# Second products of a routed-expert loop: high and low weights side by side in one 512-column product

## The chip, the cores and the metric

The kernel runs on one core of a Trainium2 chip. The metric is the device time of one execution in microseconds (us); the kernel before has a median of 1322.04 us over 3 runs.

## What is computed

The input x is (2, 2048, 256) in float32: 4096 rows of 256 features. The reference runs four residual layers one after the other: a linear attention, a mixture of experts, a causal attention, and the same mixture again with the same weights. Each mixture is

```python
xn = layernorm(layernorm(x)) * ln_gamma + ln_beta
abel_out = gelu(xn @ abel_w + abel_b)                 # dense branch, 256 -> 256
topw, topi = top_k(xn @ moe_gate_w + moe_gate_b, 2)   # 8 experts, 2 per row
h  = gelu(xn @ ew1[e] + eb1[e])                       # 256 -> 512
eo = h @ ew2[e] + eb2[e]                              # 512 -> 256
moe_out = (sum of the 2 weighted eo) @ expm(gens[0]) @ expm(gens[1]) @ expm(gens[2])
gate = sigmoid([abel_out, moe_out] @ gc_w + gc_b)
x = x + norm(x) + abel_out * (1 - gate) + moe_out * gate
```

## The kernel before, in words

**Stages.** `weights()` prepares the weights, `context()` does the linear attention, then come `mixture(0)`, `attention`, and `mixture(1)`. The three rotations are folded into the experts' second weights `ew2`. Products that must be exact use a pair of reduced-precision operands: a float32 value is kept as a high part that the engine's fast float32 format (`f32r`) holds exactly and a low part, the rest. A product is then high rows by high weights, high rows by low weights, and low rows by high weights.

**The expert loop.** Each mixture sorts its 8192 (row, expert) pairs by expert into `SLOTS` = 71 tiles of 128 rows, so there are 142 tiles in two loops (in the profile 312 to 570 us and 1005 to 1268 us). `over_tiles` runs a loop's first 7 tiles as straight code, then 7 turns of a hardware loop with 8 tiles each, then the last 8 as straight code. Engines are programmed by hand and run each its own order; semaphores bind them. For tile j:

- GpSimd (`gpsimd`, L1482 to L1496) fetches tile j+4 of x from the DRAM tensor `slots_in` once `back_ok` says that tile j is done with its ring slot, and then scatters the results of tile j (L1495) once `zy_ok` of tile j is there. It takes them in this order, so the fetch of tile j+5 stands behind the scatter of tile j.
- TensorE (`run_tiles`, L1887) does `up(j)` (6 products of 512 columns, `split` L1838, with first weights), `turn_x(j+1)` (2 transposes, L1851), `down_first(j-1)` (6 products of 256 columns), `turn_h(j)` (4 transposes, L1868) and `down_second(j-1)` (6 products of 256 columns). `split` issues L1842 (high by high), L1843 (high by low) and L1844 (low by high), for the first and for the second weights alike, each with a weight load of its own (the rows are the stationary operand, the expert's weights the moving one).
- ScalarE: Gelu of `up(j)` into `hid` (L1673), then the high part of x for tile j+1 (`high_x`, recorded as L207), then, after `turn_h`, the high part of the turned Gelu rows (recorded as L202).
- VectorE (`step`, L1388): the low part of x for tile j+1 (`copy_x`, L1357), the low part of the turned Gelu rows of tile j (L1394), and then for tile j-1: a register read of the expert number, the sum of PSUM and the expert's bias into `yr` (`results_part`, L1378), a product with the gate vector that is summed up (`gate_part`, L1385); at last two small ones for the scatter addresses of tile j+1 (`route_back`, L1366 and L1369). In the second mixture `aside` puts two products of the dense branch (L1255) behind them in tiles 1 to 6.

So the order that VectorE keeps is: L1394 of tile j, the results of tile j-1, the addresses, L1357 for tile j+2. `up(j+2)` waits for that L1357, `turn_h` waits for Gelu, and `down_first(j)` waits for L1394 of tile j.

**Banks.** The second product of tile j has the first 256 columns of PSUM bank 6 or 7 (by parity of j); the other 256 are unused.

**Memory.** `ew1` and `ew2` hold the high parts of all 8 experts. The low parts lie in DRAM and are fetched per expert by SyncE (`fetch_weights`, L1511) into one of four places, `low1_in` and `low2_in`; that of expert e+4 goes where e's was, once the tiles of e are through. `low2_in` lies under the first half of `ab`, the dense branch's result. In the second mixture `ew2` is fetched too (`high2`), since the attention used its place. `ew2` is laid out by chunk first, `[P, HC, E, C]`, so an expert's share is 4 pieces of 1 KB per partition.

Of the kernel before, what the change touches and what calls it, by code (L numbers as in the profile page):

```python
# [20 lines left out]
P = 128  # L21
# [8 lines left out]
def build(nc, d, out):  # L30
# [7 lines left out]
    NT = T // P  # L38
# [16 lines left out]
    with ctx:  # L55
# [28 lines left out]
        xh = sb("xh", [P, NT, CW])  # L84
        keys = under("keys", [P, BT // GT, 2, KC, BANK], F32)
# [3 lines left out]
        values = under("values", [P, BT // GT, 2, GT, C], F32)  # L89
        ew2 = sb("ew2", [P, HC, E, C])  # L90
# [73 lines left out]
        wqkv = flat(ab)[:, NT * C - KC * 3 * HD:].rearrange("p (c n) -> p c n", c=KC)  # L164
# [14 lines left out]
        def turn_half(pe, n, b):  # L179
            e, hs = half(n)  # L180
            for c in range(KC):
                for h in range(HH):
                    last = pe.transpose(bank[:, b, (c * HH + h) * P:(c * HH + h + 1) * P],
                                        ew2[:, hs.start + h, e, c * P:(c + 1) * P], ident[:])
            return last
# [27 lines left out]
        def weights():  # L213
# [9 lines left out]
            a3 = Arena(flat(ab)[:, GT * C:])  # L223
# [51 lines left out]
            with nc.Block() as block:  # L275
                @block.sync
                def _(sp):
# [28 lines left out]
                    for c in range(HC):  # L306
                        sp.dma_start(ew2[:, c, :, :], d["L0_ffn_ew2"][:, c * P:(c + 1) * P, :].rearrange("e p h -> p e h")
# [471 lines left out]
        ctx_arena = Arena(flat(ab))  # L779
# [21 lines left out]
        def context():  # L801
# [28 lines left out]
            with nc.Block() as block:  # L830
                @block.sync
                def _(sp):

                    sp.dma_start(turning, R.rearrange("p c j -> p (c j)")).then_inc(st_high, 16)
                    for e in range(E):
# [5 lines left out]
                        if e % 2:  # L841
                            sp.dma_start(high2[e // 2].rearrange("p (h c) -> p h c", h=HC), ew2[:, :, e // 2, :]).then_inc(st_high, 16)
# [17 lines left out]
                def _(v):  # L860
# [11 lines left out]
                    def rest_second(n):  # L872
# [4 lines left out]
                        v.tensor_tensor(rest2[n % 4], bank[:, FY[n % 2], :].rearrange("p (h c) -> p h c", h=HH), ew2[:, hs, e, :],  # L877
# [42 lines left out]
                def _(act):  # L920
# [10 lines left out]
                    def folded(n):  # L931
                        e, hs = half(n)
                        act.wait_ge(fold_Y, n + 1)
                        copy(act, f32r(ew2[:, hs, e, :]), bank[:, FY[n % 2], :].rearrange("p (h c) -> p h c", h=HH)).then_inc(fold_ok, 1)
# [101 lines left out]
        def mixture(r):  # L1036
# [86 lines left out]
            RETURNED = ((xs, xs_out), (ab, ab_out)) if r == 1 else ((xs, xs_out),)  # L1123
# [125 lines left out]
            def vector(v):  # L1249
                def dense_gate(g, some=range(GT)):  # L1250

                    v.wait_ge(gelu_ok, step_of[g] + 1)
                    for t in some:
                        after(v, zab_ok, gated(g) - GT + t)
                        v.scalar_tensor_tensor(prod, ab[:, g * GT + t, :], 1.0, gcw[:, 1, :], ALU.mult, ALU.mult,  # L1255
# [3 lines left out]
                def rest_late(n):  # L1259
# [4 lines left out]
                    v.tensor_tensor(late_rest[n % 2], bank[:, fold_bank(n), :].rearrange("p (h c) -> p h c", h=HH), ew2[:, hs, e, :],  # L1264
# [114 lines left out]

                def gate_part(j, k):  # L1380

                    v.wait_ge(y_ok, past + j + 1)
# [5 lines left out]
                def step(j, k, turn):  # L1388
# [18 lines left out]
                results_part(SLOTS - 1, (SLOTS - 1) % RING, (SLOTS - 1) // RING)  # L1407
                gate_part(SLOTS - 1, SLOTS - 1)
# [15 lines left out]
                def last_tile(g, k):  # L1424

                    if 0 <= g < NG:
# [5 lines left out]
                        src = (ab[:, g * GT + t, :], q[:, t, 0, 0:C], q[:, t, 1, 0:C])[k]  # L1432
# [65 lines left out]
            def sync(sp):  # L1498
# [7 lines left out]
                def spill_dense(p):  # L1506
                    g = ORDER[p]
                    sp.wait_ge(gelu_ok, p + 1)
                    sp.dma_start(ab_out[g], ab[:, tiles(g), :].rearrange("p t c -> p (t c)")).then_inc(spilled[g % 4], 16)

                def fetch_weights(e):  # L1511
# [58 lines left out]
                for e in range(LOWS, E):  # L1570
                    fetch_weights(e)
                    if r == 0:
# [4 lines left out]
                        sp.dma_start(high2[e].rearrange("p (h c) -> p h c", h=HC), ew2[:, :, e, :]).then_inc(late_high, 16)  # L1577
                if r == 0:
                    prepared.sync(sp)
                for g in range(LOWS):  # L1580
# [4 lines left out]
                    for o, i in RETURNED:  # L1585
                        sp.dma_start(o[:, tiles(g), :].rearrange("p t c -> p (t c)"), i[g]).then_inc(spilled[g], 16)
# [916 lines left out]
```

## Time and profile before

| | us |
|---|---|
| median of 3 runs | 1322.04 |
| lowest and highest | 1310.57, 1322.39 |
| the profiled execution's own time | 1321.78 |
| its span, first to last instruction | 1320.0 |
| first expert loop, from its first product to its last results | 312 to 570 |
| second expert loop | 1005 to 1268 |

The profile is of one execution. PE is TensorE's products, PEld its weight loads (which run beside products), DVE VectorE, ACT ScalarE, POOL GpSimd, SP SyncE. A row of the timeline has start, duration, engine, line, operation and operands, and in brackets the idle time before it with what ended it. Ends of products are modelled, so the spacing of starts is what counts. "issue" is a wait that no semaphore in the profile explains. Tensor names in rows leave out digits, so `ew` is `ew1` or `ew2`, and `low_in` is `low1_in` or `low2_in`.

### The profile page before, as it was taken

The page shows a single profiled execution, that of the slowest core. Times are in us where ns is not written, and L with a number is a line of the kernel's source. Part 1 is how long each engine was busy: PE and PEld are TensorE (multiplying, and loading weights), DVE is VectorE, ACT ScalarE, POOL GpSimd, SP SyncE. Part 2 cuts the span into 40 slices and gives each one's busy share as a digit, 9 for nine tenths or more (in the row PEclk, how much of TensorE's full clock was granted, in tenths as well). Part 3 has the DMA queues.
Part 4 walks back from the last instruction along what each step waited for, and adds up shares of the span by engine and source line. Part 5 has one row for each costly group of instructions (what it writes and reads, how often), then busy time and mean ns, then how long its engine had stood idle before and what let it go on. Part 6 is the DMA issues. An engine that isn't in the chain of part 4 may idle for free.

```text
span 1320.0 us, 25866 instructions
## 1 busy us (share of the span) xinstructions
PE 1166.6 (88%) x7208; PEld 1012.9 (77%) x7209; DVE 861.9 (65%) x2758; ACT 494.8 (37%) x961; POOL 415.0 (31%) x494
## 2 busy tenths in 40 slices
PE   7988968888999999945999989999994999999958
PEld 6746657776888899934789878888873889899947
DVE  6668767756666666655876667766672766666646
ACT  1104624244444444422333333343542444444435
POOL 3003116872444444410000000105573444444410
PEclk8998968779999999976999999998896999999979
DMA  9401314445444533360011100001247534433357
GB/s 295 140 8 65 128 64 156 160 161 181 133 140 138 162 96 88 93 224 0 1 49 49 49 20 30 1 1 65 97 165 240 188 120 124 120 105 111 105 189 256
DMA packets 72271, 149.15 MB, mean 113 GB/s; under 512 B 10918, under 2 KB 36210, under 8 KB 72186
## 3 DMA queue, kind: packets, MB, share of 16 engines
q1 hardware_dynamic: 51626, 92.87, 20.3%
q0 software_dynamic: 19776, 54.45, 13.7%
q8 instruction: 42, 0.69, 0.2%
q10 hardware_dynamic: 784, 0.79, 0.2%
q14 instruction: 43, 0.35, 0.1%
HBM read 82.63 MB, written 65.44 MB: 112 GB/s over the span
## 4 chain that ended last, share of the span: by engine, by line
PE 52%; issue 11%; DVE 7%; POOL 7%; DMA 5%; ACT 2%; POOLq 1%; SPq 1%; DVEq 0%; ACTq 0%
PE bank L2301 18%; PE bank L1842 6%; PE bank L1843 6%; PE bank L1844 6%; POOL slots_in L1474 4%; PE bank L1868 3%; PE bank L1706 3%; PE bank L1921 3%; DMA xh<-slots_in 2%; PE bank L2359 2%; POOL xh L1484 2%; PE bank L1851 2%; POOLq L1483 1%; POOL results L1495 1%; PE bank L2312 1%
## 5 line engine op out<-in xcount | busy, mean ns | idle before, releaser
L1842 PE MATMUL bank<-ew,rows 128*128 x852 | 298.2, 350 | 5.8 <-DVE rows L1357 3.8
L1843 PE MATMUL bank<-low_in,rows 128*128 x852 | 273.6, 321 | 0.0
L1844 PE MATMUL bank<-ew,rows 128*128 x852 | 272.2, 319 | 0.0
L1495 POOL DMA_INDIRECT results<-xh x142 | 143.2, 1009 | 293.7 <-DVE xh L1385 275.5
L1842 PEld LDWEIGHTS bank<-ew,rows 128*128 128x128 f32 x852 | 161.4, 189 | 17.0 <-issue 9.7
L1844 PEld LDWEIGHTS bank<-ew,rows 128*128 128x128 f32 x852 | 161.0, 189 | 11.4
L1673 ACT ACTIVATE xh<-bank 128x512 f32<-128x512 f32 x142 | 85.1, 599 | 219.3 <-PE bank L1844 219.3
L1843 PEld LDWEIGHTS bank<-low_in,rows 128*128 128x128 f32 x852 | 162.0, 190 | 6.2
L1394 DVE TENSOR_TENSOR rows<-bank,rows 128x512 fp32r<-128x512 f32 x142 | 98.2, 692 | 93.2 <-ACT rows L202 93.2
L1474 POOL DMA_INDIRECT slots_in<-xh,work x120 | 118.1, 984 | 78.3 <-DVE work L1236 44.7
L723 POOL TENSOR_TENSOR work<-work,mhalf 128x8 f32<-128x8 f32 x24 | 39.6, 1649 | 323.7 <-DVE work L716 311.0
L202 ACT ACTIVATE rows<-bank 128x512 fp32r<-128x512 f32 x142 | 85.1, 599 | 77.2 <-PE bank L1868 77.2
L2301 PE MATMUL bank<-values,shares 128*128 128x256 f32 x816 | 111.5, 288 | 1.9 <-DVE shares L2106 1.9
L2301 PE MATMUL bank<-keys,queries 128*128 128x512 f32 (+2 forms) x480 | 107.7, 377 | 0.0
L1706 PE MATMUL bank<-abw,work 128*128 128x8 f32 (+1 forms) x512 | 102.5, 348 | 3.9 <-ACT work L207 2.1
L2301 PEld LDWEIGHTS bank<-values,shares 128*128 128x128 f32 x816 | 101.7, 190 | 4.4 <-DVE shares L2106 3.6
L1706 PEld LDWEIGHTS bank<-abw,work 128*128 128x128 f32 x512 | 88.2, 216 | 13.8 <-ACT work L207 2.8
L2301 PEld LDWEIGHTS bank<-keys,queries 128*128 128x128 f32 x480 | 85.9, 195 | 13.6
L1378 DVE TENSOR_TENSOR xh<-bank,work 128x256 f32<-128x256 f32 x142 | 60.3, 425 | 49.8 <-issue 46.7
L1357 DVE SCALAR_TENSOR_TENSOR rows<-bank,rows 128x256 fp32r<-128x256 f32 x142 | 60.3, 424 | 41.4 <-ACT rows L207 38.0
L1484 POOL DMA_DIRECT2D xh<-slots_in x142 | 78.5, 553 | 27.8 <-issue 26.8
L1868 PE MATMUL bank<-ident,xh 128*128 128x128 f32 x568 | 85.6, 273 | 0.7 <-ACT xh L1673 0.7
(347 smaller groups left out, 2016.2 us busy)
## 6 DMA issues: line engine op xcount, KB each, us to landing
xh<-slots_in POOLq DMA_DIRECT2D x142, 129.0 KB, 2.6
low_in<-low SPq DMA_DIRECT2D x32, 512.0 KB, 5.0
xh<-results SPq DMA_DIRECT2D x14, 1032.0 KB, 5.4
dense<-ab SPq DMA_DIRECT2D x12, 512.0 KB, 7.2
xs<-in_L_attn_a_x_dram SPq DMA_DIRECT2D x4, 1024.0 KB, 8.4
ew<-in_L_ffn_ew_dram SPq DMA_DIRECT2D x2, 2048.0 KB, 13.3
ew<-in_L_ffn_ew_dram SPq DMA_DIRECT2D x4, 1024.0 KB, 14.4
low<-xh SPq DMA_DIRECT2D x8, 512.0 KB, 2.7
```

The costliest lines, as they stand in the source:

```text
L202: return eng.activation(o, i, ACT.Copy, scale=scale)
L1394: v.tensor_tensor(f32r(q[:, 1]), bank[:, 4 + k % 2, :], q[:, 0], ALU.subtract).then_inc(hidT_ok, 1)
L1474: pool.indirect_dma_start(out=xg, out_offset=bass.IndirectOffsetOnAxis(ap=slot[:, k, t:t + 1], axis=0), in_=place[h][:, t - h * GT, :], in ...
L1484: pool.dma_start(xr[j % RING], xg[bass.ds(at, P), :]).then_inc(x_ld[j % RING], 16)
L1495: pool.indirect_dma_start(out=yg, out_offset=bass.IndirectOffsetOnAxis(ap=back[j % RING], axis=0), in_=yr[j % RING], in_offset=None).then_ ...
L1673: act.activation(hid[k % 2], bank[:, 2 + k % 2, :], ACT.Gelu).then_inc(hid_ok, 1)
L1706: last = pe.matmul(o, of[:, c, t * P:(t + 1) * P], abw[:, c, some], start=(c == 0), stop=(c == KC - 1))
L1842: pe.matmul(o, hi, f32r(high(c)), start=(c == 0), stop=False)
L1843: pe.matmul(o, hi, f32r(low(c)), start=False, stop=False)
L1844: last = pe.matmul(o, lo, f32r(high(c)), start=False, stop=(stop and c == chunks[-1]))
L1868: last = pe.transpose(bank[:, 4 + k % 2, c * P:(c + 1) * P], hid[k % 2][:, c * P:(c + 1) * P], ident[:])
L2301: last = pe.matmul(o, f32r(left(x)), f32r(right(y)), start=(start and q == 0), stop=(stop and q == 2), skip_group_check=True)
```

## The change

The low second weights of expert e now lie four experts ahead of the high ones in one tensor: `second` has 12 places of `[HC, C]`, place e+4 is the high part of expert e (that is `ew2`), and place e takes the low part of expert e when it is fetched (for e >= 4 that overwrites the high part of expert e-4, whose tiles are done; the wait is the one of before). A strided view `second[e : e+8 : 4]` is then (low, high) of expert e. For each of the 4 chunks, one product of 512 columns takes the high rows by low and high weights into the whole bank, and one of 256 columns adds low rows by high weights to its second half. VectorE adds the two halves of the bank: the first with the bias as before, the second in a new instruction. The dense branch's rows are kept rotated by half of `ab`, so that the places of groups 0 to 3 are again those under the low weights. Weights of one expert are now contiguous.

```diff
-        low2_in = under("low2_in", [P, LOWS, HC, C], F32)
-        ab = sb("ab", [P, NT, C])
-        ew1 = sb("ew1", [P, KC, E, H])
-        ew2 = sb("ew2", [P, HC, E, C])
+        ab_ew2 = sb("ab_ew2", [P, NT * C + E * HC * C])
+        ab_flat = ab_ew2[:, 0:NT * C]
+        ab = ab_flat.rearrange("p (t c) -> p t c", c=C)
+        second = ab_ew2[:, NT * C // 2:].rearrange("p (s h c) -> p s h c", h=HC, c=C)
+        ew2 = second[:, LOWS:]
...
+        def dense_row(t):
+            return ab[:, (t + NT // 2) % NT, :]
...
+                def results_whole(j, k):
+                    v.wait_ge(y_ok, 2 * (past + j) + 1)
+                    v.tensor_tensor(yr[k][:, 0:C], yr[k][:, 0:C], bank[:, 6 + k % 2, C:], ALU.add).then_inc(y_ok, 1)
+
                 def gate_part(j, k):
-                    v.wait_ge(y_ok, past + j + 1)
+                    v.wait_ge(y_ok, 2 * (past + j) + 2)
...
                         results_part(j - 1, (k - 1) % RING, turn if k >= 1 else turn - 1)
+                        results_whole(j - 1, (k - 1) % RING)
                         gate_part(j - 1, k - 1)
...
-                    sp.dma_start(low2_in[:, e % LOWS].rearrange("p h c -> p (h c)"), low2[e]).then_inc(low_ld, 16)
+                    sp.dma_start(second[:, e].rearrange("p h c -> p (h c)"), low2[e]).then_inc(low_ld, 16)
                     if r == 1:
-                        sp.dma_start(ew2[:, :, e, :], high2[e].rearrange("p (h c) -> p h c", h=HC)).then_inc(low_ld, 16)
+                        sp.dma_start(ew2[:, e], high2[e].rearrange("p (h c) -> p h c", h=HC)).then_inc(low_ld, 16)
...
                 def down_first(j, k, e):
                     pe.wait_ge(hidT_ok, past + j + 1)
-                    since(pe, y_ok, j - 1)
+                    if not isinstance(j, int) or j >= 2:
+                        pe.wait_ge(y_ok, 2 * (past + j - 1))
                     down_part(k, e, range(HC // 2))

                 def down_part(k, e, some):
-                    o = bank[:, 6 + k % 2, 0:C]
-                    return split(o, hidT[k % 2], some, lambda c: ew2[:, c, bass.ds(e, 1), :],
-                                 lambda c: low2_in[:, bass.ds(e % LOWS, 1), c, :], some[-1] == HC - 1)
+                    o = bank[:, 6 + k % 2, :]
+                    for c in some:
+                        hi, lo = (f32r(hidT[k % 2][:, q, c * P:(c + 1) * P]) for q in range(2))
+
+                        def both():
+                            return pe.matmul(o.rearrange("p (q c) -> p q c", q=2), hi, f32r(second[:, bass.ds(e, 2, LOWS), c, :]),
+                                             start=(c == 0), stop=(c == HC - 1), skip_group_check=True)
+
+                        if c < HC - 1:
+                            both()
+                        last = pe.matmul(o[:, C:], lo, f32r(second[:, bass.ds(e + LOWS, 1), c, :]), start=False, stop=False,
+                                         skip_group_check=True)
+                        if c == HC - 1:
+                            last = both()
+                    return last
```

The rest of the change is indices: the folding of rotations, the stores and loads of `ew2`, and the readers of `ab` take the new layout.

## Rows read from the trace of the kernel before

**Rows 1.** The page's part 1: busy time of TensorE, share, instructions.
```profile
PE 1166.6 (88%) x7208; PEld 1012.9 (77%) x7209; DVE 861.9 (65%) x2758; ACT 494.8 (37%) x961; POOL 415.0 (31%) x494
```

**Rows 2.** Busy us (and instructions) of each engine in stretches; then clock, DMA share, GB/s.
```profile
1130.00:1180.00 50.00, 49.92 (x345) 45.14 (x344) 31.98 (x99) 20.95 (x43) 22.32 (x29) 1.00 0.42 126
1180.00:1230.00 50.00, 49.98 (x342) 45.07 (x341) 31.85 (x99) 20.89 (x43) 22.15 (x30) 1.00 0.32 95
```

**Rows 3.** The chain of work that ended last, 450 to 460 us: start, us, what.
```profile
450.85 0.23 PE bank L1842
...
452.22 0.22 PE bank L1851 x2
...
453.16 0.44 PE bank L1868 x4
```

**Rows 4.** Weight loads in order of time, one tile of the first loop.
```profile
355.56 0.19 PEld L1842 LDWEIGHTS bank<-ew,rows 128*128 128x128 f32 x1
...
357.90 0.45 PEld L1868 LDWEIGHTS bank<-ident,xh 128*128 128x128 f32 x4
358.32 0.19 PEld L1842 LDWEIGHTS bank<-ew,rows 128*128 128x128 f32 x1
...
359.02 0.19 PEld L1842 LDWEIGHTS bank<-ew,rows 128*128 128x128 f32 x1
```

**Rows 5.** ScalarE in order of time, the same tile.
```profile
357.26 0.60 ACT L1673 ACTIVATE xh<-bank 128x512 f32<-128x512 f32 x1 [1.50 <-PE bank L1844]
357.75 0.38 ACT L207 ACTIVATE rows<-bank 128x256 fp32r<-128x256 f32 x1
```

**Rows 6.** VectorE in order of time, that tile and the end of the one before it.
```profile
354.74 0.25 DVE L1369 SCALAR_TENSOR_TENSOR xh<-xh,work 128x1 int32<-128x1 f32 x1 [0.15 <-DVE xh L1366]
354.92 0.42 DVE L1357 SCALAR_TENSOR_TENSOR rows<-bank,rows 128x256 fp32r<-128x256 f32 x1
355.79 0.69 DVE L1394 TENSOR_TENSOR rows<-bank,rows 128x512 fp32r<-128x512 f32 x1 [0.45 <-ACT rows L202]
356.73 0.42 DVE L1378 TENSOR_TENSOR xh<-bank,work 128x256 f32<-128x256 f32 x1 [0.25 <-issue]
...
357.85 0.25 DVE L1369 SCALAR_TENSOR_TENSOR xh<-xh,work 128x1 int32<-128x1 f32 x1 [0.15 <-DVE xh L1366]
358.16 0.42 DVE L1357 SCALAR_TENSOR_TENSOR rows<-bank,rows 128x256 fp32r<-128x256 f32 x1
359.26 0.69 DVE L1394 TENSOR_TENSOR rows<-bank,rows 128x512 fp32r<-128x512 f32 x1 [0.68 <-ACT rows L202]
```

**Rows 7.** The page's part 5: busy, mean ns, idle before and its cause.
```profile
L1378 DVE TENSOR_TENSOR xh<-bank,work 128x256 f32<-128x256 f32 x142 | 60.3, 425 | 49.8 <-issue 46.7
```

**Rows 8.** VectorE in order of time at the second loop's start.
```profile
1018.07 0.69 DVE L1394 TENSOR_TENSOR rows<-bank,rows 128x512 fp32r<-128x512 f32 x1 [0.68 <-ACT rows L202]
...
1020.79 0.42 DVE L1357 SCALAR_TENSOR_TENSOR rows<-bank,rows 128x256 fp32r<-128x256 f32 x1
...
1025.09 0.69 DVE L1394 TENSOR_TENSOR rows<-bank,rows 128x512 fp32r<-128x512 f32 x1 [0.40 <-ACT rows L202]
```

**Rows 9.** Weight loads in order of time, the same place.
```profile
1021.40 0.19 PEld L1842 LDWEIGHTS bank<-ew,rows 128*128 128x128 f32 x1
```

**Rows 10.** Waits of weight loads: 311 to 572 us, then 1004 to 1268 us: us, times, longest.
```profile
PEld bank L1851 <- DMA xh<-slots_in: 4.6, 4, 1.8
...
PEld bank L1851 <- DMA xh<-slots_in: 3.8, 6, 1.2
```

**Rows 11.** The chain of work that ended last, 433 to 443 us.
```profile
435.07 6.42 DMA xh<-slots_in
```

**Rows 12.** DMA issues by line: count, KB each, median us to landing.
```profile
low_in<-low SPq DMA_DIRECT2D x32, 512.0 KB, 5.0
...
ew<-high SPq DMA_DIRECT2D x8, 512.0 KB, 7.1
```

More of the change, by code:

```diff
@@ L162, in flat4, with dense_rows @@
             return t[:].rearrange("p a b c -> p (a b c)")
-        wqkv = flat(ab)[:, NT * C - KC * 3 * HD:].rearrange("p (c n) -> p c n", c=KC)
+        def dense_rows(first, many=1):
+            at = (first + NT // 2) % NT
+            return ab[:, at:at + many, :]
+        def dense_row(t):
+            return ab[:, (t + NT // 2) % NT, :]
+        wqkv = ab_flat[:, NT * C - KC * 3 * HD:].rearrange("p (c n) -> p c n", c=KC)
         R = flat(xh)[:, 0:KC * C].rearrange("p (c j) -> p c j", c=KC)
@@ L183, in turn_half @@
                     last = pe.transpose(bank[:, b, (c * HH + h) * P:(c * HH + h + 1) * P],
-                                        ew2[:, hs.start + h, e, c * P:(c + 1) * P], ident[:])
+                                        ew2[:, e, hs.start + h, c * P:(c + 1) * P], ident[:])
             return last
@@ L841, in _ @@
                         if e % 2:
-                            sp.dma_start(high2[e // 2].rearrange("p (h c) -> p h c", h=HC), ew2[:, :, e // 2, :]).then_inc(st_high, 16)
+                            sp.dma_start(high2[e // 2].rearrange("p (h c) -> p h c", h=HC), ew2[:, e // 2]).then_inc(st_high, 16)
                     sp.wait_ge(st_high, 16 * (1 + FOLDS // 2))
@@ L933, in folded @@
                         act.wait_ge(fold_Y, n + 1)
-                        copy(act, f32r(ew2[:, hs, e, :]), bank[:, FY[n % 2], :].rearrange("p (h c) -> p h c", h=HH)).then_inc(fold_ok, 1)
+                        copy(act, f32r(ew2[:, e, hs, :]), bank[:, FY[n % 2], :].rearrange("p (h c) -> p h c", h=HH)).then_inc(fold_ok, 1)
                     def mixed(b):
@@ L1122, in mixture @@
             BACK = 32
-            RETURNED = ((xs, xs_out), (ab, ab_out)) if r == 1 else ((xs, xs_out),)
+            RETURNED = ((lambda g: xs[:, tiles(g), :], xs_out), (lambda g: dense_rows(g * GT, GT), ab_out))[0:1 + r]
             if r == 1:
@@ L1263, in rest_late @@
                     after(v, late_st[n % 2], 16 * (n // 2))
[L1264 removed]
+                    v.tensor_tensor(late_rest[n % 2], bank[:, fold_bank(n), :].rearrange("p (h c) -> p h c", h=HH), ew2[:, e, hs, :],
                                     ALU.subtract).then_inc(rest_ok, 1)
@@ L1407, in vector @@
                 results_part(SLOTS - 1, (SLOTS - 1) % RING, (SLOTS - 1) // RING)
+                results_whole(SLOTS - 1, (SLOTS - 1) % RING)
                 gate_part(SLOTS - 1, SLOTS - 1)
@@ L1508, in spill_dense @@
                     sp.wait_ge(gelu_ok, p + 1)
-                    sp.dma_start(ab_out[g], ab[:, tiles(g), :].rearrange("p t c -> p (t c)")).then_inc(spilled[g % 4], 16)
+                    sp.dma_start(ab_out[g], dense_rows(g * GT, GT).rearrange("p t c -> p (t c)")).then_inc(spilled[g % 4], 16)
                 def fetch_weights(e):
@@ L1576, in sync @@
                         sp.wait_ge(fold_ok, LATE_FOLDS)
-                        sp.dma_start(high2[e].rearrange("p (h c) -> p h c", h=HC), ew2[:, :, e, :]).then_inc(late_high, 16)
+                        sp.dma_start(high2[e].rearrange("p (h c) -> p h c", h=HC), ew2[:, e]).then_inc(late_high, 16)
                 if r == 0:
@@ L1585, in sync @@
                     for o, i in RETURNED:
-                        sp.dma_start(o[:, tiles(g), :].rearrange("p t c -> p (t c)"), i[g]).then_inc(spilled[g], 16)
+                        sp.dma_start(o(g).rearrange("p t c -> p (t c)"), i[g]).then_inc(spilled[g], 16)
                 for k in range(RING):
@@ L1630, in folded_late @@
                     act.wait_ge(fold_Y, n + 1)
-                    copy(act, f32r(ew2[:, hs, e, :]), bank[:, fold_bank(n), :].rearrange("p (h c) -> p h c", h=HH)).then_inc(fold_ok, 1)
+                    copy(act, f32r(ew2[:, e, hs, :]), bank[:, fold_bank(n), :].rearrange("p (h c) -> p h c", h=HH)).then_inc(fold_ok, 1)
                 def gelu(p):
@@ L1635, in gelu @@
                         act.wait_ge(ab_ps, p)
-                        act.activation(ab[:, tiles(ORDER[p - 1]), :].rearrange("p t c -> p (t c)"), psum(4, 2), ACT.Gelu
+                        act.activation(dense_rows(ORDER[p - 1] * GT, GT).rearrange("p t c -> p (t c)"), psum(4, 2), ACT.Gelu
                                        ).then_inc(gelu_ok, 1)
@@ L1940, in attention @@
             w.take(GT * (CW - C))
-            for later in (flat(ab), flat4(ew2)):
-                spare = Arena(later[:, NT * C // 2:])
+            for at in (NT * C // 2, NT * C + E * HC * C // 2):
+                spare = Arena(ab_ew2[:, at:at + NT * C // 2])
                 y_at.append(spare.take(GT, 2 * CW))
```

19 lines of the change are left out of this document (11 added, 8 removed).

## The prediction

> **What bounds the kernel now.** I read the busy times first, then the stretches, then the chain, and last single tiles in order of time.
>
> TensorE is busy for 88% of the span [rows 1]. In the expert loops it is busy all the time: 49.92 and 49.98 of 50 us, at the full granted clock (1.00, the level of 2.4 GHz), while VectorE has 32 of 50, ScalarE 21 and GpSimd 22 [rows 2]. A tile has 24 products, so 345 and 342 of them in 50 us are 14.3 tiles: 3.48 us each. The two loops take some 258 and 263 us of the 1320, and only there does the change touch work that the chain passes.
>
> The chain of one tile adds up: from 450.85 to 452.22 six products of 512 columns take 1.37 us (0.228 each); two transposes take 0.22; from 452.44 to 453.16 six products of 256 columns take 0.72 (0.12 each); four transposes 0.44 [rows 3]. With the second six that is 1.37 + 0.22 + 0.72 + 0.44 + 0.72 = 3.47 us.
>
> "TensorE is full" is not the whole story, though. In an ordinary tile the Gelu (L1673) starts at 357.26 and ends at 357.86 [rows 5], and the weight loads of turn_h start at 357.90 [rows 4]. So turn_h starts the moment Gelu lets it. And the low part of x (L1357) ends at 358.58 [rows 6], with the first load of up at 359.02, behind down_second's six loads from 358.32 on and 3.46 after the up before (355.56) [rows 4]: VectorE is 0.44 us ahead of what TensorE needs. At the second loop's start, where VectorE has more to do, that load follows L1357's end by 0.19 (1020.79 + 0.42 = 1021.21, then 1021.40) [rows 8, 9]; so 0.19 is what the handover needs, and VectorE's true slack is 0.25 us per tile. That small number decides this case.
>
> **TensorE's part.** Per chunk, two products of 256 columns (2 × 0.12) become one of 512 (0.228), and the third stays: 0.36 becomes 0.348. Per tile 4 × 0.012 = 0.05 us; with the rounding of the rows 0.04 to 0.05. The number of columns stays 3072, and the weight loads saved (4 of 24) ran beside products. No row shows a 512-column product whose operand comes in two pieces 16 KB apart, nor a short product between long ones. Bounds: if the pieces cost as two products do, the gain is 0; if the short product shrinks to a transpose's spacing (0.11), it is 4 × 0.022 = 0.09. I take 0.04, nearest to the row of the contiguous 512. Of it, half falls into down_first, ahead of turn_h, which waits for Gelu and not for TensorE. So only down_second's half counts: 0.02 us per tile, 142 tiles: 3 us at best, 6 if Gelu's limit were not there. The address registers of the new view are computed ahead of products that fill the engine; I cost them at nothing, and a wait in front of L1842 would show it otherwise.
>
> The Trainium skill has a rule that would make the loads themselves the bound: "TensorE: Matmul & The Clock Gate", the mechanism in the part on packing, has a weight load overlap products in flight only when it goes to another row group (the same page also lets a load go to a background buffer). Our loads all use the full array. It is a rival below.
>
> **VectorE's part.** results_whole is a new instruction with the shape of L1378: 0.425 us [rows 7], and it waits for its forerunner, as L1385 does today (L1378's 0.42 and 0.04 more). I take 0.46 per tile. It stands between L1394 and L1357, and behind it are queued gate_part (then GpSimd's scatter), route_back (then GpSimd's fetch), and L1357 (then up). Bounds: 0.42 without a gap, 0.5 with one.
>
> What that does: from L1394 at 355.79 to L1369 at 357.85 is 2.06 us, and L1357 can start 0.18 after L1369 does (354.74 to 354.92) [rows 6], so 2.24. (In that tile it started at 358.16 only, since ScalarE's high part of x ended at 358.13 [rows 5]; this wait goes.) That tile's wait for the register read ("issue") was 0.25, the mean is 49.8 / 142 = 0.35 [rows 7]: on average 2.34. Afterwards it is 2.80. Where does the loop close? L1394 of tile j, L1357 for j+2, up(j+2), Gelu, turn_h, L1394 of j+2: a ring through two tiles. The second loop's start measures it with VectorE as the bound: L1357 starts 1020.79 - 1018.07 = 2.72 after L1394, and the L1394 two tiles on comes 1025.09 - 1018.07 = 7.02 after [rows 8]. So with 2.80 the ring takes 7.10, a tile 3.55. Before it is 3.475; TensorE alone would now need 3.455. The new bound is thus the ring, and an ordinary tile gets 0.07 to 0.08 us longer. With the short register read of rows 6 the ring is 7.00 (3.50, +0.025); with reads of 0.45 it is 3.60 (+0.125). I take 0.07.
>
> Sum over tiles. Of 142, 14 are turns of the hardware loop, 10 wait for x [rows 10], 6 have the dense branch aside; the rest, some 110, are ordinary: 110 × 0.07 = 7.7 us. In the 6 tiles with the dense branch VectorE is the bound already, and its 0.46 counts over two tiles: 6 × 0.23 = 1.4; some of them also wait for x, so 1.
>
> **GpSimd and x.** GpSimd fetches tile j+5 behind the scatter of tile j, which waits for gate_part. Today x sometimes comes late: 4 waits of 4.6 us in all, and 6 of 3.8 [rows 10], when a fetch takes 6.42 us to land [rows 11]. The fetch is now asked for 0.46 later, and three longer tiles give 0.2 back: 0.25 on each of 10 waits, 2.5 us. Bounds: 0 where TensorE is late for another reason, 5 where each counts in full.
>
> **Ends.** In each loop's last tile nothing hides the addition: 2 × (0.46 - 0.04) = 0.8 us.
>
> **Moved layouts.** high2 now goes in pieces of 4 KB, not 1 KB. Its 8 loads of 512 KB land in 7.1 us, where those of low weights, already in long pieces, take 5.0 [rows 12]. They are asked for an expert ahead, so I count only less crowding for x: -0.5, bounds 0 and -2. The wait of down for bank 6 or 7 (both halves read) comes a tile after the additions and costs nothing. The rotated dense rows keep every wait.
>
> Sum: 7.7 + 1 + 2.5 + 0.8 - 0.5 = 11.5 us on the profiled execution's 1321.8, which is 0.3 under the median: 1333 us, 0.9% more.
>
> **Rivals.**
> 1. *TensorE stays the bound.* If the register read is ready sooner in the new order (it has longer to come), or the handover needs less than 0.19, the ring is under 6.91 and only TensorE's gain is left: 3 to 6 us off, some 1 to 3 us back at the ends and on x: 1318. For it: VectorE's load, 0.46 more in 3.475, is 77%, and 0.25 of slack is more than half covered. Against it: the ring as measured. This is the side of "not slower"; it decides when L1394 to L1357 stays under some 2.6 us.
> 2. *VectorE's delay runs deeper.* Reads of 0.45 and a fetch delay that counts in full: 110 × 0.12 + 1.4 + 5 + 0.8 = 20 us, 1342. For it: a mean of 0.35 beside reads of 0.25 means that some take 0.45. Against it: in a stall VectorE catches up.
> 3. *The weight loads are the bound.* If loads could not run beside products, each of the 4 saved would give back what a transpose takes, 0.11: 4 × 0.11 × 142 = 62 us, 1260. Against it: the 24 loads of a tile at 0.19 [rows 4] would fill 4.6 us, and a tile takes 3.47; and products of 512 and 256 columns, 0.228 and 0.12 apart, follow their columns [rows 3]. The Trainium skill's rule above would lead here; the trace disagrees with it.
> 4. *The change doesn't do what it says*: the product of two pieces runs as two, gain 0, everything on VectorE as above: 1333 again, so it can't be told from the time, only from the spacing.
>
> **Chances.** Forecast 0.60, rival 1 0.24, rival 2 0.11, rival 3 0.03, something else 0.02. The time of the likeliest is 1333. The range takes in the bounds of the forecast, rival 1 and most of rival 2: 1315 to 1345. What a measurement of this kernel can tell from no change is about 1%, 13.2 us, and the forecast's +11.5 lies just inside it: same gets rival 1 and over half of the forecast's cases, 0.56; slower the others and rival 2, 0.38; faster rival 3 and half of the unknown, 0.06.
>
> **What the profile after would show.** Right: L1394 spaced some 3.55 us in ordinary tiles, in place of 3.475; the load of up 0.2 us behind L1357's end, in place of 0.44; VectorE some 36 to 37 of 50 us in the loops; TensorE's idle time in front of L1842 grown, released by L1357; the long product spaced 0.23 and the short 0.12; waits for x of 10 to 11 us in place of 8.4. Wrong: a spacing of 3.45 with turn_h 0.05 behind Gelu (rival 1), or shorter gaps around the short products than 0.11 (then TensorE gains more than I gave it).

## The result, and the profile after

| | median, us | lowest to highest | runs |
|---|---|---|---|
| before, beside it | 1320.31 | 1310.57 to 1323.14 | 20 |
| after | 1328.45 | 1318.35 to 1336.62 | 20 |

The ratio is 1.0063, with a 95% interval of 1.0043 to 1.0084: 8 us more, where 11.5 were forecast. The profiled execution took 1328.49 us with a span of 1326.9, against 1321.78 and 1320.0.

Part 1 of the page of after (busy us, share of the span, instructions) answers to [rows 1]:

```profile
PE 1167.9 (88%) x6640; PEld 978.7 (74%) x6641; DVE 917.3 (69%) x2900; ACT 494.9 (37%) x961; POOL 415.0 (31%) x494
```

Weight loads are down three points, VectorE is up. Neither share says which way the time goes; TensorE's is unchanged. The stretches of the second expert loop (columns as in [rows 2]) say more:

```profile
1130.00:1180.00 50.00, 49.96 (x281) 41.45 (x280) 37.17 (x112) 20.61 (x42) 21.56 (x28) 1.00 0.37 119
1180.00:1230.00 50.00, 49.91 (x281) 41.41 (x280) 36.94 (x113) 20.61 (x42) 21.36 (x29) 1.00 0.33 101
```

A tile now has 20 products, so 562 in 100 us are 28.1 tiles, 3.56 us each; before it was 687 / 24 = 28.6 tiles, 3.49 each. TensorE counts as full in both. VectorE went from 32 to 37 of 50. The chain, in one tile of that loop:

```profile
1194.05 0.45 PE bank L1863
1194.51 0.23 PE bank L1864
...
1195.66 0.22 PE bank L1872 x2
1195.88 0.23 PE bank L1905
1196.11 0.12 PE bank L1910
1196.23 0.23 PE bank L1905
1196.46 0.12 PE bank L1910
1196.58 0.44 PE bank L1889 x4
1197.02 0.24 PE bank L1905
1197.25 0.23 PE bank L1910 x2
1197.49 0.23 PE bank L1905
1197.72 0.23 PE bank L1863
```

The product of 512 columns on the two pieces (L1905) takes 0.23, the short one between long ones (L1910) 0.12: the new products cost what they should. From 1194.28 (one product of 0.23 is in the 0.45; the other 0.22 is a wait) to 1197.72 a tile is 3.44 us.

That 0.22 is the kind of wait that the forecast is about. VectorE around it, in order of time (start, us, engine, line; in brackets the idle time before it and its releaser). L1413 is the low part of the Gelu rows (L1394 before), L1392 and L1397 the two additions, L1404 the gate, L1380 and L1383 the addresses, L1371 the low part of x (L1357 before):

```profile
1190.56 0.69 DVE L1413 TENSOR_TENSOR rows<-bank,rows 128x512 fp32r<-128x512 f32 x1 [0.45 <-ACT rows L216]
1191.69 0.42 DVE L1392 TENSOR_TENSOR xh<-bank,work 128x256 f32<-128x256 f32 x1 [0.44 <-issue]
...
1193.44 0.42 DVE L1371 SCALAR_TENSOR_TENSOR rows<-bank,rows 128x256 fp32r<-128x256 f32 x1
1194.02 0.69 DVE L1413 TENSOR_TENSOR rows<-bank,rows 128x512 fp32r<-128x512 f32 x1
1194.96 0.42 DVE L1392 TENSOR_TENSOR xh<-bank,work 128x256 f32<-128x256 f32 x1 [0.25 <-issue]
1195.42 0.42 DVE L1397 TENSOR_TENSOR xh<-xh,bank 128x256 f32<-128x256 f32 x1
1195.87 0.43 DVE L1404 SCALAR_TENSOR_TENSOR xh<-xh,gcw 128x256 f32<-128x256 f32 x1
...
1196.53 0.25 DVE L1383 SCALAR_TENSOR_TENSOR xh<-xh,work 128x1 int32<-128x1 f32 x1 [0.15 <-DVE xh L1380]
1196.71 0.42 DVE L1371 SCALAR_TENSOR_TENSOR rows<-bank,rows 128x256 fp32r<-128x256 f32 x1
1197.69 0.69 DVE L1413 TENSOR_TENSOR rows<-bank,rows 128x512 fp32r<-128x512 f32 x1 [0.55 <-ACT rows L216]
...
1201.13 0.69 DVE L1413 TENSOR_TENSOR rows<-bank,rows 128x512 fp32r<-128x512 f32 x1 [0.33 <-ACT rows L216]
...
1204.67 0.69 DVE L1413 TENSOR_TENSOR rows<-bank,rows 128x512 fp32r<-128x512 f32 x1 [0.42 <-ACT rows L216]
```

And the load of up, in the weight loads:

```profile
1194.01 0.19 PEld L1863 LDWEIGHTS bank<-ew,rows 128*128 128x128 f32 x1 [0.27 <-issue]
...
1197.33 0.19 PEld L1863 LDWEIGHTS bank<-ew,rows 128*128 128x128 f32 x1
```

L1371 ends at 1193.86 and the load starts 0.15 behind it; in [rows 4, 6] that was 0.44. This L1371 belongs to the ring that starts at 1190.56. The register read takes 0.44 there, L1371 comes 1193.44 - 1190.56 = 2.88 behind L1413, and the L1413 two tiles on comes 1197.69 - 1190.56 = 7.13 behind it: the ring of the forecast. The next L1371 is 1196.71 - 1194.02 = 2.69 behind its L1413, with a read of 0.25. It ends at 1197.13, and TensorE does not wait for it: its products follow one another without a gap until up starts at 1197.72. The ring behind that closes again, with a read of 0.25: 1204.67 - 1197.69 = 6.98. Two tiles of TensorE's own take 6.88.

So the loss isn't spread evenly. From 1194.02 on the tiles take 3.67, 3.44, 3.54 and 3.44, and in the later turns of a loop this comes back with every turn of eight tiles. Whoever reads a single tile can hit any of them.

The second addition starts 0.46 behind the first. The line of L1392 on the page (idle before it at the end), which answers to [rows 7]:

```profile
L1392 DVE TENSOR_TENSOR xh<-bank,work 128x256 f32<-128x256 f32 x142 | 60.3, 425 | 39.8 <-issue 36.4
```

The idle time there fell from 49.8 us to 39.8, or from 0.35 to 0.28 a tile. This is the register read of the expert's number ahead of the addition. Of the 108 tiles outside the first and the last eight of each loop, it took 0.22 to 0.28 in 42 and 0.38 or more in 48 before; after, in 83 and in 17. The tile right behind a turn of the hardware loop, 12 of the 108, has 11 of these 17.

The waits of the weight loads in the two loops, 311 to 580 us and 1004 to 1275 us (us, times, longest), answer to [rows 10]:

```profile
PEld bank L1863 <- issue: 8.2, 20, 2.3
PEld bank L1872 <- DMA xh<-slots_in: 8.2, 6, 2.2
...
PEld bank L1863 <- issue: 11.0, 28, 1.5
PEld bank L1872 <- DMA xh<-slots_in: 1.9, 4, 0.7
```

In the whole run L1863 waits 48 times for 19.2 us, where the same load waited 18 times for 9.7 before. "Issue" names no releaser here; that it is L1371 is read from the times above. The waits for x are 10.1 us in 10, as against 8.4 in 10.

The DMA issues (count, KB each, us to landing), which answer to [rows 12]:

```profile
low_in<-low SPq DMA_DIRECT2D x16, 512.0 KB, 4.2
ab_ew<-low SPq DMA_DIRECT2D x16, 512.0 KB, 5.6
ab_ew<-high SPq DMA_DIRECT2D x8, 512.0 KB, 6.5
```

**Where the 8 us are.** For this I took the starts of VectorE's low part of the Gelu rows (one a tile) in each trace, and sorted the spacings of the two loops of 71 tiles: the 14 in all that hold a turn of the hardware loop (every eighth); the ordinary ones (outside the first and the last eight, under 3.8 us); the stalls among them (3.8 and more; their excess is over 3.475). A loop's time goes from its first to its last such start. The tables below all come from this sorting, each from one trace, so differences of a few tenths of a microsecond between them say little.

| | loop 1, us | loop 2, us | mean at a turn | ordinary: n, mean | stalls: n, excess | first 8 of loop 2 |
|---|---|---|---|---|---|---|
| before | 251.2 | 249.6 | 3.88 | 89, 3.490 | 7, 6.3 | 29.6 |
| after | 257.9 | 253.2 | 4.05 | 84, 3.516 | 12, 11.6 | 30.9 |

In each loop the first of its seven turns is the entry. That of the second loop, 4.24 before and 4.85 after, falls among the tiles with the dense branch and stands in two columns, under turns and under the first 8. The other 13 turns take 3.85 before and 3.99 after.

The loops take 6.7 and 3.6 us more. That is 10.3, of which the span shows 6.9: the stretch between the loops is 3.7 us shorter in this one trace (448.2 before, 444.5 after). Here it is before and then after (columns as in [rows 2]):

```profile
566.80:1015.00 448.20, 374.84 (x2439) 332.85 (x2439) 293.12 (x907) 157.28 (x277) 93.90 (x87) 0.91 0.20 69
```

```profile
574.00:1018.50 444.50, 369.75 (x2434) 328.14 (x2435) 293.53 (x908) 157.28 (x277) 93.36 (x87) 0.93 0.19 69
```

TensorE does the same work there in 5.1 us less, at a mean granted clock of 0.93, not 0.91. So the shorter stretch goes with the clock of that execution; that the change has no part in it is not shown.

### The profile page after: what moved, and what is told of

It reads as the page before. It is cut to its first block, busy times and chain, and to the rows that moved or that the text cites. A ratio compares the mean times of both kernels' runs of the same rounds, so it can differ in the third digit from the quotient of the medians.

```text
span 1326.9 us, 25096 instructions
## 1 busy us (share of the span) xinstructions
PE 1167.9 (88%) x6640; PEld 978.7 (74%) x6641; DVE 917.3 (69%) x2900; ACT 494.9 (37%) x961; POOL 415.0 (31%) x494
## 4 chain that ended last, share of the span: by engine, by line
PE 54%; issue 10%; POOL 7%; DVE 6%; DMA 5%; ACT 1%; POOLq 1%; SPq 1%; DVEq 0%; ACTq 0%
PE bank L2336 18%; PE bank L1905 7%; POOL slots_in L1495 5%; PE bank L1863 4%; PE bank L1910 4%; PE bank L1865 3%; PE bank L1864 3%; PE bank L1889 3%; PE bank L1956 3%; PE bank L2394 2%; PE bank L1727 2%; PE bank L1872 2%; DMA xh<-slots_in 2%; POOL xh L1505 1%; DMA ab_ew<-high 1%
## 5 line engine op out<-in xcount | busy, mean ns | idle before, releaser
L1905 PE MATMUL bank<-ab_ew,rows 128*128 x568 | 242.6, 438 | 1.6 <-DVE rows L1413 1.6
L1413 DVE TENSOR_TENSOR rows<-bank,rows 128x512 fp32r<-128x512 f32 x142 | 98.2, 691 | 62.2 <-ACT rows L216 61.0
L1910 PE MATMUL bank<-ab_ew,rows 128*128 x568 | 136.7, 281 | 0.0
L1863 PE MATMUL bank<-ew,rows 128*128 x284 | 118.5, 417 | 6.3 <-DVE rows L1371 4.7
L1905 PEld LDWEIGHTS bank<-ab_ew,rows 128*128 128x128 f32 x568 | 107.4, 189 | 8.0 <-issue 2.3
L2336 PE MATMUL bank<-under_ew,shares 128*128 128x256 f32 x816 | 111.4, 288 | 1.9 <-DVE shares L2141 1.9
L1910 PEld LDWEIGHTS bank<-ab_ew,rows 128*128 128x128 f32 x568 | 108.0, 190 | 6.3
L1865 PE MATMUL bank<-ew,rows 128*128 x284 | 112.4, 396 | 0.0
L1864 PE MATMUL bank<-low_in,rows 128*128 x284 | 112.0, 394 | 0.0
L2336 PEld LDWEIGHTS bank<-under_ew,shares 128*128 128x128 f32 x816 | 101.6, 190 | 4.3 <-DVE shares L2141 3.5
L1727 PE MATMUL bank<-abw,work 128*128 128x8 f32 (+1 forms) x512 | 98.4, 339 | 3.9 <-ACT work L221 2.1
L1727 PEld LDWEIGHTS bank<-abw,work 128*128 128x128 f32 x512 | 84.9, 209 | 12.9 <-ACT work L221 2.8
L1392 DVE TENSOR_TENSOR xh<-bank,work 128x256 f32<-128x256 f32 x142 | 60.3, 425 | 39.8 <-issue 36.4
```

The costliest lines, as they stand in the source:

```text
L1413: v.tensor_tensor(f32r(q[:, 1]), bank[:, 4 + k % 2, :], q[:, 0], ALU.subtract).then_inc(hidT_ok, 1)
L1727: last = pe.matmul(o, of[:, c, t * P:(t + 1) * P], abw[:, c, some], start=(c == 0), stop=(c == KC - 1))
L1863: pe.matmul(o, hi, f32r(high(c)), start=(c == 0), stop=False)
L1864: pe.matmul(o, hi, f32r(low(c)), start=False, stop=False)
L1865: last = pe.matmul(o, lo, f32r(high(c)), start=False, stop=(stop and c == chunks[-1]))
L1905: return pe.matmul(o.rearrange("p (q c) -> p q c", q=2), hi, f32r(second[:, bass.ds(e, 2, LOWS), c, :]), start=(c == 0), stop=(c == HC - 1 ...
```

## The experiments

The runs come in three sets, each on a chip of its own with the kernel before beside them. The kernel before took 1344.08 us (24 runs) in the first set, 1321.76 in the second and 1319.79 in the third, so only ratios are compared across sets.

### First set: product or addition, addresses or fetch

**before_sum_twice** puts the second addition, and nothing else of the change, into the kernel before:

```diff
+ def results_again(j, k):
+     e = texp_now[0]
+     v.wait_ge(y_ok, 2 * (past + j) + 1)
+     v.tensor_tensor(yr[k][:, 0:C], bank[:, 6 + k % 2, 0:C], bias[:, bass.ds(e, 1), :], ALU.add).then_inc(y_ok, 1)
...
+         results_again(j - 1, (k - 1) % RING)
```

> The kernel before with the sum of bank and bias done twice, one behind the other, as the changed kernel has two sums; products and layout as before. Theory A: as slow as the changed kernel or some 3 to 6 us slower, 1328 to 1335, ratio about 1.009; tiles of 3.5 to 3.7 us appear between those of 3.47, and waits for x grow. Rival B: within 2 us of the kernel before, ratio 1.000.

**no_second_sum** is the kernel after without it. The one addition reads the half `C:` of the bank, so the high rows by low weights are left out of the result:

```diff
- v.tensor_tensor(yr[k][:, 0:C], bank[:, 6 + k % 2, 0:C], bias[:, bass.ds(e, 1), :], ALU.add)
+ v.tensor_tensor(yr[k][:, 0:C], bank[:, 6 + k % 2, C:], bias[:, bass.ds(e, 1), :], ALU.add)
...
-         results_whole(j - 1, (k - 1) % RING)
```

> The changed kernel without the new VectorE instruction: the second half of the bank is added to the bias, and the first half (high rows by low weights) is left out of the result. Theory A (the added instruction lengthens VectorE's part of the two-tile ring, and TensorE's products gain a little): 3 to 6 us under the kernel before, ratio about 0.997; ordinary tiles all at 3.44 us in place of 3.475. Rival B (the 512-column product with two pieces, or the new layout, costs the time): still about 8 us over the kernel before, ratio 1.006.

Measured: before_sum_twice 1.0058 (1.0037 to 1.0080), no_second_sum 0.9984 (0.9970 to 0.9999). A stretch of the second loop, of before_sum_twice and then of no_second_sum:

```profile
1160.00:1210.00 50.00, 49.92 (x337) 44.61 (x336) 37.24 (x112) 20.60 (x42) 21.66 (x28) 1.00 0.42 125
```

```profile
1160.00:1210.00 50.00, 49.96 (x285) 41.90 (x284) 32.16 (x100) 20.59 (x42) 21.66 (x28) 1.00 0.43 129
```

The first has 24 products a tile, 337 / 24 = 14.04 tiles; the second 20, 285 / 20 = 14.25. The addition alone, with the old products and the old layouts, gives the time and the tile of the kernel after (1.0063, 14.05); the new products and layouts without it give a little less than the kernel before. So the loss is VectorE's second addition, and the wide product with its layouts is worth 0.2% (0.01 to 0.3%), less than the 3 to 6 us expected.

| | loop 1 | loop 2 | at a turn | ordinary | stalls | first 8 |
|---|---|---|---|---|---|---|
| before_sum_twice | 255.8 | 256.1 | 4.09 | 84, 3.517 | 12, 10.5 | 31.8 |
| no_second_sum | 251.0 | 248.0 | 3.84 | 85, 3.459 | 11, 8.9 | 29.2 |

**after_addresses_early** takes work out from between L1413 and L1371: route_back for the next tile moves from the end of the step to right behind the low part of the next x, ahead of L1413.

```diff
+ route_back(j + 1, k + 1, turn + (k + 1) // RING)
...
- if not is_last(j):
-     route_back(j + 1, k + 1, turn + (k + 1) // RING)
```

> The changed kernel with the two address instructions of a tile moved from behind the gate product to right behind that tile's low part of x, where VectorE waits for ScalarE. Theory A: the ring loses 0.49 us of VectorE and gained 0.46, so the bound goes back to TensorE and the Gelu: 1318 to 1322, ordinary tiles 3.44, ratio about 0.999; waits for x stay, since the fetch stands behind the scatter. Rival C (only the later scatter and fetch of x cost the time, not the ring): within 2 us of the changed kernel, 1327 to 1330, ratio 1.006.

Measured: 1.0058 (1.0037 to 1.0078), a miss, though its ordinary tiles are 3.412, the shortest of all. (That is under TensorE's 3.44, since tiles right behind a stall come quicker, down to 3.03.) A new line in its waits ate the gain:

```profile
DVE xh L1380 <- DMA results<-xh: 18.2, 14, 2.4
```

The addresses have four slots, and one is free only when the scatter of four tiles ago has landed. At the end of a step it has; a part of a tile earlier, 14 times not, and VectorE stands 18.2 us in all, with the low part of the Gelu rows and all that follows it behind the addresses. The excess of its stalls is 20.6 us.

**after_fetch_early** lets GpSimd ask for x of tile j + 5 ahead of the scatter of tile j:

```diff
+ pool.wait_ge(back_ok, past + 1)
+ fetch(RING)
...
-     if j + RING < SLOTS:
-         pool.wait_ge(back_ok, past + j + 1)
-         fetch(j + RING)
+     if j + RING + 1 < SLOTS:
+         pool.wait_ge(back_ok, past + j + 2)
+         fetch(j + RING + 1)
```

> The changed kernel with GpSimd's order turned: the fetch of tile j+5 goes ahead of the scatter of tile j, not behind it. Theory A: waits for x (16 us over both loops in the profile after, 8 in the one before) nearly go, but tiles of 3.5 to 3.7 stay: 1316 to 1322, ratio about 0.999. Rival C: the same time off, and all tiles without a wait for x at 3.44. Rival D (x is late for DMA traffic alone, whenever it is asked for): 1327 to 1330.

Measured: 1.0011 (1.0000 to 1.0022), a little more than the 0.999 of theory A. Its stalls are 5 with 3.0 us of excess, but its ordinary tiles are 3.531 and its turns 4.02: the waits for x are gone and the ring is not.

### Second set: the same with room, and on the kernel before

**after_addresses_8** moves the addresses and gives them eight slots; the suffix **_fetch** adds the early fetch; **before_...** are the same edits on the kernel before.

```diff
- back = [x.take(1, dt=I32) for _ in range(RING)]
+ back = [x.take(1, dt=I32) for _ in range(2 * RING)]
...
- after(v, y_st[b], 16 * turn)
+ after(v, y_st[b], 16 * (turn - 1))
```

> The changed kernel with the address instructions right behind the low part of x, as in the run with early addresses, but with 8 address slots in place of 4, so that VectorE waits for the scatter seven tiles back and not for the one three back. That run had all ordinary tiles at 3.44 us, yet 14 new waits of 18.2 us in all for a scatter to land. Theory A (ring): these waits go, ordinary tiles stay at 3.44, waits for x stay near those of the changed kernel or shrink: ratio 0.995 to 1.000 to the kernel before. Rival E (VectorE's order does not matter, since late fetches of x cost what the ring gives): ratio 1.005 as the changed kernel.

> The same with the fetch of tile j+5 ahead of the scatter of tile j. Theory A: ordinary tiles 3.44 and nearly no wait for x: 10 to 14 us under the kernel before, ratio 0.990 to 0.993, 17 to 20 us under the changed kernel. Rival E: no better than the changed kernel with the early fetch alone, ratio 1.001.

> The kernel before with both moves (early addresses with 8 slots, early fetch). Theory A: waits for x go and ordinary tiles stay at 3.475, TensorE's own time: ratio 0.993 to 0.996, that is 4 to 5 us slower than the changed kernel with both moves, which is what the 512-column product is worth once VectorE has room. Rival: equal to it within 2 us, then the wide product is worth nothing.

> The kernel before with the early fetch alone. If x waits are all that it removes (about 8 to 12 us of waits in the profile), ratio 0.992 to 0.995, ordinary tiles 3.475. The changed kernel with the same move stood at 1.0011: the difference, 0.6 to 0.9%, is then the ring's price alone.

| | ratio | 95% | loop 1 | loop 2 | at a turn | ordinary | stalls | first 8 |
|---|---|---|---|---|---|---|---|---|
| after_addresses_8 | 1.0002 | 0.9975 to 1.0029 | 254.2 | 250.5 | 4.09 | 86, 3.454 | 10, 11.8 | 29.6 |
| after_addresses_8_fetch | 0.9931 | 0.9908 to 0.9955 | 246.4 | 247.6 | 4.08 | 94, 3.450 | 2, 0.9 | 30.7 |
| before_addresses_8_fetch | 0.9922 | 0.9891 to 0.9953 | 247.4 | 247.2 | 3.93 | 93, 3.480 | 3, 1.6 | 28.9 |
| before_fetch_early | 0.9950 | 0.9922 to 0.9978 | 246.8 | 247.2 | 3.90 | 95, 3.483 | 1, 0.4 | 29.0 |

With slots enough the early addresses bring the ordinary tile of the kernel after to 3.45, TensorE's own time, and the whole back to the kernel before. The early fetch gives both kernels the same again: 1.0063 to 1.0011 in after (after_fetch_early) and 1 to 0.9950 in before. The two loops go from 511.1 to 504.1 and from 500.8 to 494.0, 7 us each. One expectation here is a miss: with both moves the kernel before was to be 4 to 5 us slower than the kernel after, and it is not; its rival, a wide product worth nothing, fits.

### Third set: the register read ahead of the wait

**after_read_early** moves only VectorE's read of the expert's number, from between L1413 and the addition to ahead of L1413, where VectorE waits for ScalarE anyway:

```diff
+ e = expert_of(j - 1) if not isinstance(j, int) or j >= 1 else None
...
- e = v.value_load(texp[0:1, j:j + 1] if isinstance(j, int) else texp[0:1, bass.ds(j, 1)],
-                  min_val=0, max_val=E - 1)
```

> The changed kernel with VectorE's register read of the expert number moved from between the low part of the Gelu rows and the first sum to right behind the low part of x, where VectorE waits for ScalarE anyway. The read's 0.25 us leave the ring, scatters and fetches keep their order. Theory A (a two-tile ring through VectorE sets the ordinary tile): tiles of 3.5 to 3.7 us get fewer and shorter (ring 6.5 to 6.8 us, TensorE needs 2 x 3.44), ratio 1.001 to 1.003 in place of 1.006. Rival F (the move of the addresses helped only because it signals the fetch earlier): no change from the changed kernel, 1.005 to 1.007.

> The changed kernel with the early read and the early fetch. Theory A: x waits gone and the ring short: 0.993 to 0.996. Rival F: 1.001, as with the early fetch alone.

> The changed kernel with all three moves (read, addresses with 8 slots, fetch). The turns of the hardware loop took 4.00 us with the moved addresses and 3.87 in the kernel before; if VectorE's chain makes that difference, the shorter chain brings them back to 3.87 or less: 0.989 to 0.992. If the moves have nothing left to give, 0.993 as before.

> The kernel before with the early read and the early fetch. VectorE has 0.25 us of slack there already, so the read should give nothing in ordinary tiles (3.475): 0.994 to 0.996, as with the early fetch alone. Then the difference to the changed kernel with the same moves is the price or the worth of the wide product with its second sum.

| | ratio | 95% | loop 1 | loop 2 | at a turn | ordinary | stalls | first 8 |
|---|---|---|---|---|---|---|---|---|
| after_read_early | 0.9988 | 0.9964 to 1.0011 | 250.8 | 248.8 | 3.89 | 85, 3.462 | 11, 8.2 | 30.1 |
| after_read_fetch | 0.9929 | 0.9898 to 0.9959 | 246.4 | 247.2 | 3.91 | 93, 3.465 | 3, 1.4 | 30.2 |
| after_read_addresses_8_fetch | 0.9952 | 0.9930 to 0.9974 | 247.3 | 248.6 | 4.08 | 93, 3.450 | 3, 1.9 | 32.1 |
| before_read_fetch | 0.9956 | 0.9932 to 0.9980 | 248.6 | 247.7 | 3.91 | 93, 3.480 | 3, 2.0 | 29.7 |

VectorE of after_read_early in order of time (L1416 is the low part, L1394 the first addition here):

```profile
1194.01 0.69 DVE L1416 TENSOR_TENSOR rows<-bank,rows 128x512 fp32r<-128x512 f32 x1 [0.68 <-ACT rows L216]
1194.62 0.41 DVE L1394 TENSOR_TENSOR xh<-bank,work 128x256 f32<-128x256 f32 x1
...
1196.36 0.42 DVE L1371 SCALAR_TENSOR_TENSOR rows<-bank,rows 128x256 fp32r<-128x256 f32 x1
1197.48 0.69 DVE L1416 TENSOR_TENSOR rows<-bank,rows 128x512 fp32r<-128x512 f32 x1 [0.70 <-ACT rows L216]
```

The addition starts 0.61 behind the low part, not 0.94, and the low part has 0.7 us of waiting for ScalarE ahead of it in both tiles, not 0.55, 0.33 or none. The spacing is 3.47. All additions are still there; 0.3 us of slack was enough to take the whole loss back, more than the 1.001 to 1.003 expected. The kernel before has nothing to win by the same move: with the early fetch it stands at 0.9956 with the early read and at 0.9950 without. So the read counts only where it is in the ring that closes last. The three moves together are a miss: 0.989 to 0.992 was expected, and the turns were to fall to 3.87.

## Why the prediction was right, and where its sizes were off

The forecast was 1333 us, within 1% of before; it came to 1328.45 by the median, and +8 where the sum was +11.5. The mechanism is the one forecast, the ring through VectorE, and before_sum_twice and after_read_early show it from both sides: put the addition in and the loss is there, give VectorE 0.3 us back and it is gone.

**Right, by its steps.** The second addition costs 0.46 behind its forerunner. The products are spaced 0.23 and 0.12, a chunk 0.35, and TensorE's own tile is 3.44 to 3.45 (forecast 3.455). VectorE is busy 37 of 50 us (forecast 36 to 37). The load of up stands 0.15 behind the L1371 that it waits for, no longer 0.44 (the forecast took 0.19 for the handover). The ring through two tiles is 7.13 with a read of 0.44, from 2.88 in VectorE, and 6.98 with a read of 0.25, from 2.69; the forecast has 7.10 from 2.80 and 7.00 from 2.70. What L1413 of two tiles on is behind L1371, 4.25 and 4.29, is thus the 4.30 that was read at the second loop's start. In the last tile of the first loop nothing hides the addition (VectorE in order of time), 0.46 as priced:

```profile
576.61 0.42 DVE L1392 TENSOR_TENSOR xh<-bank,work 128x256 f32<-128x256 f32 x1 [0.48 <-PE bank L1905]
577.07 0.42 DVE L1397 TENSOR_TENSOR xh<-xh,bank 128x256 f32<-128x256 f32 x1
```

**The ordinary tile was overpriced, its sum was not.** The forecast took +0.07 on 110 tiles, 7.7 us. The sorting gives +0.026 (3.490 to 3.516); with the waits for x out of the way in both it is +0.048 (3.483 to 3.531). The term that was mis-sized is the register read: I carried the mean of 0.35 from [rows 7] into the new order. It became 0.25 in most tiles, which is the case that the forecast gave as its bound, "the ring is 7.00 (3.50, +0.025)", and some 0.45 in the tile behind a turn, which makes the tile of 3.67. But the sorting leaves out spacings from 3.8 on, and late tiles of the ring are among them. Taken together, the 96 tiles outside the turns and the first and last eight of the loops take 7.5 us more (0.08 a tile), and 7.0 more with the early fetch, where no weight load waits for x in either kernel. So 7.7 was near as a sum. How the late tiles beyond 3.8 come about was not separated, and in this the sum owes something to luck.

**The turns of the hardware loop were left out.** I had counted 110 ordinary tiles and taken nothing for the 14 turns. They went from 3.88 to 4.05: 14 × 0.17 = 2.4 us, of which 0.6 is the entry of the second loop. The other 13 went from 3.85 to 3.99. The addition alone does it (4.02 in before_sum_twice), and the early read takes it back (3.80). A turn in after, VectorE in order of time:

```profile
1186.57 0.69 DVE L1413 TENSOR_TENSOR rows<-bank,rows 128x512 fp32r<-128x512 f32 x1 [0.33 <-ACT rows L216]
...
1189.69 0.42 DVE L1371 SCALAR_TENSOR_TENSOR rows<-bank,rows 128x256 fp32r<-128x256 f32 x1 [0.34 <-issue]
1190.56 0.69 DVE L1413 TENSOR_TENSOR rows<-bank,rows 128x512 fp32r<-128x512 f32 x1 [0.45 <-ACT rows L216]
```

VectorE's own turn stands between the addresses and L1371, 0.34 us with no releaser named: there the ring gets longer by itself. As I read it, the slack that is gone in the ordinary tile covered a part of this before; no run tried the turn alone.

**The tiles with the dense branch aside.** The first eight of the second loop take 1.3 us more (29.6 to 30.9; 29.0 to 31.1 in the pair with the early fetch), where 1 was forecast for six such tiles. Of the 1.3, 0.6 is the loop's entry again, already counted with the turns.

**The waits for x cost the change next to nothing.** Forecast 2.5, bounds 0 to 5. The waits of L1872 for x grew by 1.7 us, and the excess of stalls by 5.3, in which late tiles of the ring are counted too. But the early fetch, which takes these stalls away, gains 7 us in both kernels alike. With it the loops of the two kernels are 10.1 us apart, without it 10.3. So it is the lower bound: x is late by much the same in both.

**The moved layouts gave nothing that can be seen.** The high weights land in 6.5 us, not 7.1, but of the low weights the second ones take 5.6 where all took 5.0 before, and packets fell from 72271 to 66127. no_second_sum, with the new layouts and no more work on VectorE, has 11 stalls where the kernel before has 7 (on another chip): no relief for x to be seen.

**The total.** The loops took 10.3 us more: 7.5 in those 96 tiles, 2.4 at the turns, 0.6 in the other first tiles of the second loop, and 0.2 less at the rest. The forecast had 11.5 by another split: no turns, and 2.5 for x. The 20 runs a side say 8.1 us, and the one pair of traces 6.9, with 3.4 less outside the loops. That the traces' total for the loops comes so near 11.5 is in part luck.

Rival 1 (TensorE stays the bound, 1318) named its point well: it decides when L1413 to L1371 stays under some 2.6 us. It was 2.69. The early read makes it 1196.36 - 1194.01 = 2.35, and the kernel comes out at 1317.1, 0.9988: rival 1, made true by one moved instruction. Rival 2 (1342) needed reads of 0.45, and they came in 17 of 108 tiles only. Rival 3 (weight loads as the bound, 1260) is out: with four of 24 loads gone TensorE's own tile is 0.03 us shorter, not 0.44. By the Trainium skill, "TensorE: Matmul & The Clock Gate", section "The mechanism", a weight load overlaps products in flight only when it goes to another row group. The runs disagree: 20 full-array loads of 0.19 are 3.8 us, and they stand beside products in a tile of 3.44. Rival 4 is out by the spacing of 0.23 for the two pieces.

**What the change is worth if VectorE has room.** With the early read and fetch the pair is 0.9929 after to 0.9956 before; with the early addresses and fetch 0.9931 to 0.9922. The intervals overlap in both: the wide product is neither shown to gain nor to lose then, though the ordinary tile is 0.015 to 0.03 us shorter. The best versions, 0.992 to 0.993, beat both kernels, and of the gain over the kernel before most is the early fetch (0.9950), which has nothing to do with the change.

**Open.** Why the register read took 0.25 in some tiles and 0.45 or more in others before, and 0.25 in nearly all but the tile behind a turn after. Why the three moves together (0.9952) are no better than two. The intervals overlap (0.9930 to 0.9974 against 0.9898 to 0.9959), so that they are worse is not shown; the turns stand at 3.98 without the second loop's entry, where after_read_fetch has 3.83, and that entry, 5.35 against 5.02, is also in its first eight tiles of 32.1. Nothing was run to separate these. What makes tiles beyond 3.8 where x is not late.

## What to carry to other kernels

When a change takes work from the full engine and adds an instruction to another, compare the addition with the slack of that engine at that place (end of its result to the first use, less what the handover needs), not with its busy share: VectorE was at 64%, its slack was 0.25 us, and 0.46 was added. Look for the ring, count it over as many tiles as it has buffers, make sure that the engine does wait at the end of the piece that you measure, and price the turns of the hardware loop as a kind of tile of their own. Before giving such a change up, look for something in that ring that needn't be there: a register read moved into a wait took the whole loss back.

## What the runs showed that I had not expected

A register read between two VectorE instructions costs 0.25 us or more of the engine's time and shows only as "issue"; moved to where the engine waits anyway it costs nothing, 0.75% here (1.0063 to 0.9988, on two chips). Addresses computed a part of a tile earlier ran into their own four slots, 14 waits of 18.2 us in all, where the traces of before and after show none at this place. And the order of two GpSimd instructions, a fetch behind a scatter that waits for VectorE, was worth 0.5% on the kernel before (0.9950, 0.9922 to 0.9978), nearly as much as the change that was studied cost (0.6%).
